# A row of shifts placed by a DMA transfer, score tiles of every fourth target, and side work in other places, in a fused graph-attention layer on one core

## The reference

```python
h = jnp.maximum(_layernorm(x), 0.0)
hs = layer_norm(h, ln1_scale, ln1_bias)            # sources, masked by nodemask
ht = layer_norm(h_target, ln1_scale, ln1_bias)     # targets
q = (ht @ Wq + bq).reshape(T, H, HD) / sqrt(HD)
k = (hs @ Wk + bk).reshape(S, H, HD)
v = (hs @ Wv + bv).reshape(S, H, HD)
logits = einsum('thd,shd->hts', q, k)
logits = where(adj[None] != 0, logits, -1e30)
probs = softmax(logits, axis=-1)
ctx = einsum('hts,shd->thd', probs, v).reshape(T, D)
ht = ht + ctx @ Wo + bo
ht = layer_norm(ht, ln2_scale, ln2_bias)
out = x + ht + gelu(ht @ W1) @ W2
```

## Time and profile before

| | |
|---|---|
| median of 3 runs | 741.07 us (739.25 to 742.01) |
| the profiled execution | 739.28 us, span of its instructions 737.5 us |
| busy, share of the span | PE 91%, DVE 77%, POOL 72%, ACT 61% |
| before unit 0's first score product | 75.66 us |
| units 0 to 31 | 75.66 to 636.57 us |
| behind unit 31 | 100.93 us |

### The profile page before, as it was taken

One profiled execution on the slowest core, in us unless ns is written; L12 is line 12 of the kernel. 1 busy time (PEld: TensorE's weight loads), 2 busy tenths in 40 slices (PEclk: granted clock), 3 DMA queues, 4 the chain that ended last, 5 costly groups with the idle time before them and its releaser, 6 DMA issues.

```text
span 737.5 us, 20293 instructions
## 1 busy us (share of the span) xinstructions
PE 674.4 (91%) x8386; PEld 482.6 (65%) x8386; DVE 569.3 (77%) x962; ACT 450.3 (61%) x806; POOL 533.4 (72%) x504
## 2 busy tenths in 40 slices
PE   4777989999999999969989998799899988889998
PEld 4345656776776777647767766577577756548667
DVE  5858499989889977988899789786677984564651
ACT  4532456666776656667766666775566776775650
POOL 3440299988999977859999688697987998752430
PEclk9999799999999999999999999999999999999999
DMA  8284501103000100210011002020000000000001
GB/s 301 59 246 106 191 30 59 60 31 101 2 2 31 59 30 31 68 63 3 2 59 57 32 31 58 2 97 21 2 2 2 3 2 2 1 1 22 23 16 57
DMA packets 20796, 36.22 MB, mean 49 GB/s; under 512 B 2752, under 2 KB 13280, under 8 KB 20704
## 3 DMA queue, kind: packets, MB, share of 16 engines
q1 hardware_dynamic: 20704, 34.92, 15.1%
HBM read 26.49 MB, written 2.10 MB: 39 GB/s over the span
## 4 chain that ended last, share of the span: by engine, by line
PE 63%; DVE 16%; POOL 10%; issue 6%; ACT 4%; DMA 1%; SPq 0%; DVEq 0%; ACTq 0%
PE score L412 26%; PE early L412 16%; PE ctx L412 12%; POOL prob_lo L1303 7%; DVE early L1100 7%; PE aux L412 7%; DVE prob_lo L1108 3%; ACT prob L817 1%; DVE st_x L1029 1%; POOL w_f L1343 1%; POOL nT L1337 1%; DVE half_max L1100 1%; DVE q_stage L1126 1%; DMA node_i<-in_nodemask 1%; POOL tgt L1307 0%
## 5 line engine op out<-in xcount | busy, mean ns | idle before, releaser
L1303 POOL TENSOR_TENSOR prob_lo<-prob 128x512 f16<-128x512 f32 x384 | 439.9, 1169 | 96.0 <-ACT prob L817 94.8
L817 ACT ACTIVATE prob<-score 128x512 f32<-128x512 f32 x512 | 304.6, 597 | 182.2 <-PE score L412 175.6
L412 PE MATMUL score<-nidentb,mask_nat 128*128 128x128 bf16 x2048 | 201.0, 221 | 9.2 <-ACT prob L817 7.9
L412 PE MATMUL early<-kT,qT 96*128 96x512 f16 x512 | 193.5, 384 | 15.4 <-DVE half_max L1100 15.1
L412 PEld LDWEIGHTS ctx<-v_sb,prob 128*128 128x128 bf16 x2048 | 159.8, 98 | 69.9 <-ACT raw L839 14.6
L412 PE MATMUL ctx<-v_sb,prob 128*128 128x65 f16 x2048 | 192.9, 193 | 10.3 <-POOL prob_lo L1303 5.7
L412 PE MATMUL score<-qT,kT 97*128 97x512 f16 x512 | 198.5, 388 | 0.0
L1100 DVE CUSTOM_DVE_ANT_0 early<-early,mask_nat,half_max 128x1024 f32<-128x1024 f32 x128 | 164.1, 1287 | 43.0 <-PE early L412 41.5
L412 PE MATMUL ctx<-v_sb,prob_lo 128*128 128x65 f16 x2048 | 191.8, 193 | 0.0
L1100 DVE CUSTOM_DVE_ANT_0 early<-early,mask_nat 128x1024 f32<-128x1024 f32 x128 | 156.8, 1231 | 32.1 <-PE early L412 30.7
L412 PEld LDWEIGHTS ctx<-v_sb,prob_lo 128*128 128x128 f16 x2048 | 143.9, 98 | 49.2 <-issue 5.4
(11 more groups left out here) (163 smaller groups left out, 626.9 us busy)
## 6 DMA issues: line engine op xcount, KB each, us to landing
adj_in<-in_adj SPq DMA_DIRECT2D x26, 512.0 KB, 3.8
qT<-q_stage SPq DMA_DIRECT2D x48, 64.0 KB, 2.0
kT<-mask_nat SPq DMA_DIRECT2D x48, 64.0 KB, 2.1
raw<-in_x SPq DMA_DIRECT2D x4, 512.0 KB, 5.6
tgt<-in_L_gnn_h_target SPq DMA_DIRECT2D x4, 512.0 KB, 4.8
prob<-in_adj SPq DMA_DIRECT2D x4, 512.0 KB, 7.4
nT<-in_L_gnn_W SPq DMA_DIRECT2D x2, 1024.0 KB, 8.3
mask_nat<-in_x SPq DMA_DIRECT2D x1, 2048.0 KB, 8.1
```

Source lines behind the costliest of these rows:

```text
L412: return nc.tensor.matmul(dst, w, m, start=start, stop=stop, **more)
L817: nc.scalar.activation(prob[:, n % SLOTS, :], score[n % 2][:, :], ACT.Exp).then_inc(exp_done, 1)
L1303: nc.gpsimd.tensor_tensor(prob_lo[:, n % SLOTS, :], prob[:, n % SLOTS, :], prob_hi(n % SLOTS), ALU.subtract).then_inc(lo_sem["pool"], 1)
```

## The change

It does several things. The row of shifts: the four products and the copy of each unit are gone. ScalarE writes the negated maxima as a compact 128x4 tile (two buffers, by unit parity), and SyncE issues a transfer of it into row 96 of `qT` (`place_shifts`); the next unit's first score product waits for its landing. For the transfer to write the row in order, column `t` of the maxima must hold targets `4*p+t`: the adjacency is loaded so (every fourth row), the early products take every fourth column of `qT` as weights, and the mask products write every fourth column of the score bank.

The side work: in the start, GpSimd masks block 1 of the sources before it norms block 3, the first key projection uses another bank, and the placements are issued head group by head group. `sum_values` stands before unit 0; `up_bias` goes from unit 24 to unit 1; `scale_weight` goes from GpSimd in unit 25 to VectorE in units 2 to 5; `weight_high` and `weight_low` are spread from unit 3 on. Six of the eight mask halves change place, the second norm is one to two units earlier, the turning of the first feed-forward block goes from r = 7 to r = 5. In the last two units VectorE makes eight low halves in place of four. In the tail, turning the last context and multiplying it by Wo are put among the up products.

```diff
-SHIFT_STEP = 8
-MEAN_AT = {(0, 1): 0, (0, 4): 1}
+SHIFT_STEP = 6
-MASK_DVE = [(0, 6), (1, 2), (1, 7), (2, 4), (3, 1), (4, 1), (4, 5), (5, 2)]
+MASK_DVE = [(0, 6), (2, 1), (2, 4), (2, 7), (3, 7), (4, 3), (4, 7), (5, 3)]
+LOAD_AT = [(0, 0), (0, 0), (0, 1), (2, 0), (2, 1), (3, 0), (4, 0), (4, 1)]
-NORM_AT = [(0, 4), (0, 7), (1, 3), (1, 6)]
+NORM_AT = [(0, 5), (1, 1), (1, 3), (1, 5)]
-DVE_LO = (2, 6, 10, 14)
+DVE_LO = [(2, 6, 10, 14)] * (UNITS - 2) + [tuple(range(1, STEPS, 2))] * 2
...
+BIAS_AT = STEPS + 2
...
-                    sp.dma_start(adj_home(k, i), adj[k * TB + t * P:k * TB + (t + 1) * P, h * HALF:(h + 1) * HALF]).then_inc(
+                    sp.dma_start(adj_home(k, i), adj[k * TB + t:(k + 1) * TB:TT, h * HALF:(h + 1) * HALF]).then_inc(
...
+                def place_shifts(u):
+
+                    sp.wait_ge(shift_ready, u + 1)
+                    sp.dma_start(q_block(u // H)[SHIFT_ROW:SHIFT_ROW + 1, u % H, :], shift[:, u % 2, :]).then_inc(shift_in[u % 2], 16)
...
-                    last = mm(early[e % 2][:, i * TB:(i + 1) * TB], q_block(k)[0:ROWS, h, t * P:(t + 1) * P],
+                    last = mm(early[e % 2][:, i * TB:(i + 1) * TB], q_block(k)[0:ROWS, h, t::TT],
...
-                        pe.wait_ge(aux_done, AUX["shift", u] + 1)
+                        pe.wait_ge(shift_in[u % 2], 16 * (u // 2 + 1))
...
-                        mm(score[n % 2][:, t * P:(t + 1) * P], mask_nat[:, k % 2, t, m * P:(m + 1) * P], nidentb[:, :],
+                        mm(score[n % 2][:, t::TT], mask_nat[:, k % 2, t, m * P:(m + 1) * P], nidentb[:, :],
...
-                def shift_row(u):
...
-                    for t in range(TT):
-                        last = mm(aux[0:SHIFT_ROW + 1, t * P:(t + 1) * P], shift[:, t, :], ident16[:, :], True, True)
-                    last.then_inc(aux_ready, 1)
...
-                def row_out(u):
-                    job_here("shift", u)
-                    nc.scalar.activation(q_block(u // H)[SHIFT_ROW:SHIFT_ROW + 1, u % H, :], aux[SHIFT_ROW:SHIFT_ROW + 1, :],
-                                         ACT.Copy).then_inc(aux_done, 1)
...
-                            if r == 5 and s == 15:
+                            if r == 4 and s == 1:
                                 row_deviation(k - 1, lead_width(k - 1))
-                            if r == 6 and s in (2, 4, 7, 11):
+                            if r == 5 and s in (2, 4, 7, 11):
                                 second_norm(k - 1, (2, 4, 7, 11).index(s))
...
-                            if r == 5 and 3 <= j < 3 + TT:
+                            if r == 3 and 3 <= j < 3 + TT:
                                 lead_stats(k - 1, j - 3, j == 2 + TT)
-                            if r == 6 and j == 1:
+                            if r == 4 and j == 2:
                                 lead_scale(k - 1, lead_width(k - 1))
```

More of the change, by code:

```diff
@@ L77, in aux_job @@
     k, r = divmod(u, H)
[L78 to L81, removed]
     if k + 1 < NTB and (r, s) in QT_AT:
@@ L102, in aux_numbers @@
 def aux_numbers():
-    jobs = [("shift", 0)] + [aux_job(u, s) for u in range(UNITS) for s in range(STEPS) if aux_job(u, s)]
+    jobs = [("mean", 0), ("mean", 1)] + [aux_job(u, s) for u in range(UNITS) for s in range(STEPS) if aux_job(u, s)]
     jobs += [("cT", NTB - 1, c) for c in range(DC)] + [("wo", NTB - 1, i) for i in range(TT // 2)]
@@ L120, in pairs_at, with lo_counts @@
     return range(first, min(first + 1, UNITS * PAIRS))
[L123 to L128, removed]
+def lo_counts():
+    count, done = {"dve": 0, "pool": 0}, []
+    for n in range(TILES):
+        who = "dve" if n % STEPS in DVE_LO[n // STEPS] else "pool"
+        count[who] += 1
+        done.append((who, count[who]))
+    return done
+LO_DONE = lo_counts()
 def lo_here(u, j):
-    first = [m for m in DVE_LO if m < 3] if u == 0 and j == 0 else []
-    soon = [u * STEPS + m for m in range(2 * j + 3, 2 * j + 5) if m % STEPS in DVE_LO]
-    return first + [n for n in soon if n < TILES]
+    first = [n for n in range(3)] if u == 0 and j == 0 else []
+    soon = range(u * STEPS + 2 * j + 3, u * STEPS + 2 * j + 5)
+    return [n for n in [*first, *soon] if n < TILES and LO_DONE[n][0] == "dve"]
 def adj_use(k, i):
@@ L299, in prob_hi, with proj_bank @@
             return prob[:, slot, :].bitcast(BF16).rearrange("p (t two) -> p t two", two=2)[:, :, 1]
+        def proj_bank(g, m):
+            return early[0][:, m * TB:(m + 1) * TB] if g == 1 else (ctx, aux)[m][:, :]
         def value_bank(i):
@@ L666, in _ @@
                             early_scores(e, s % 2)
-                        if aux_job(u, s) == ("shift", u + 1):
-                            shift_row(u + 1)
-                        if k == 0 and (r, s) in MEAN_AT:
-                            sum_values(MEAN_AT[r, s])
+                        if n == BIAS_AT:
+                            up_bias()
                         if k + 1 < NTB:
@@ L925, in _ @@
                     high_values(i)
+                act.wait_ge(q_first, FIRST)
+                act.wait_ge(q_placed[0], REST)
+                for g in range(2):
+                    mean_out(g)
                 negated(0)
-                row_out(0)
                 for n in range(AHEAD):
```

230 lines of the change are left out of this document (126 added, 104 removed).

## The result

The changed kernel takes 801.13 us, median of 4 runs (800.13 to 801.39), beside 740.63 for the kernel before, measured with it: a ratio of 1.0814 [1.0791, 1.0837], slower. The forecast of 712 fell; the time is that of the first rival, 797. In the profiled execution the span grew from 737.5 to 799.6 us.

The account below looks back on a forecast made before the run. TensorE was taken to bound a plain unit (14.91 us), other engines some units. Against the profiled 739.28 us the terms summed to -26.9, giving 712 us; its own range was 700 to 726, stretched to 806 to include half-rate mask products.

Parts of the forecast that it names:

- first rival: Mask products of every tile run at half rate: 0.20 us a tile over 512 tiles, total 797 us; chance 0.36.
- The stride in PSUM and in the weights: Mask products writing, and early weights read, every fourth column: taken to cost nothing, though called the weak point.
- tight spots of the queue: Next block's shift row, behind query placements at r = 5, lands slightly late: 0.5 on each of three, +1.5 us.
- start, to the first score product: Before unit 0: shorter TensorE stream, but first shift row behind 60 placements; -1 us, between +3 and -3.
- unit 0: First unit loses the two mean sums, 16 products of 256 columns each, on busy TensorE: -3 us.
- units 1 and 2: `up_bias` enters unit 1 (19.9 us), three mask halves and weight scaling fill unit 2 (18.1): +5 us.
- units 3 to 7: Weights' low halves on GpSimd, 1.2 us each, raise it to 15.0 against 14.9: nothing, with the shift's saving.
- blocks 1 and 2: Middle blocks: mask halves, norms, statistics and square root change units; -3.7 and -4.6, together -8.3 us.
- units 24 to 27: Last block's first half: unit 24 loses `up_bias` (-4.3 us), unit 25 two scalings (-4.9), the other two -0.4.
- units 28 to 31: Last four units fall from 63.5 to 56.5 us, the final two having nearly no early products: -7.0.
- tail: After the last unit: turned-context work among the up products removes about 4.5 of 6.7 us TensorE idle: -4.5.
- The wait on the transfer: Each unit's shift row lands in 2.0 to 2.6 us, hidden within 3.3, except three tight places: +1.5 us.

Follow-up runs that it names:

- experiment 1: Kernel after, with the four mask products writing 128 neighbouring columns of the score bank again, transfers and strided early weights kept: 726.98 us, ratio 0.9807.
- experiment 3: Kernel before, with only the mask products changed to write every fourth column of the score bank: 817.14 us, ratio 1.1016.
- experiment 8: Kernel after, with the four shift products and the copy put back and tiles in the order of before, leaving the moved work alone: 723.74 us, ratio 0.9767.
- experiment 11: experiment 8 with the tail of before put back: 722.77 us, ratio 0.9735.

## Why the prediction was wrong, and where it was right

The forecast fell by one step, "The stride in PSUM and in the weights": "I take nothing, since the mask, score and early products all go at the column rate of their clock". None of those rows has a gap in its output, so they could say nothing on it, and the Trainium skill's rule that was cited against the choice is the one that held for this stride. Measured it is 0.18 for four mask products and 0.03 on the score product behind them, 74 us in all, from experiments 1 and 3. The range of 700 to 806 holds the 801 only because it had been stretched to the rival; the forecast itself had the wrong sign.

Rival 1 had the mechanism, with 0.20 a tile, and its plain unit of 17.9 is the 17.94 measured. That its 797 comes so near is in part luck. It stands on the 712, which is 15 below the 727 of the kernel without the stride, and it adds 85 for the stride, which is 11 above the 74: it took 17 of 102 as hidden, where the runs show 21.7 of 95.9 by busy times and some 33 of 107 by the spacing of starts. The other half of the step was right: the weights' stride costs nothing that shows.

The rest can be read in experiments 1 and 8, which have the moved work without the stride. The table gives differences to the profiled execution of before in us, by the borders of units; the three measured columns each sum to the difference of the spans, but for rounding. The start of experiment 1 is its first score product at 79.70.

| stretch | forecast | exp. 1 (transfer) | exp. 8 (products) | after |
|---|---|---|---|---|
| tight spots of the queue | +1.5 | in the units | in the units | in the units |
| start, to the first score product | -1 | +4.0 | -1.3 | +4.2 |
| unit 0 | -3 | -2.5 | -4.7 | -0.1 |
| units 1 and 2 | +5 | +4.0 | +6.4 | +8.3 |
| units 3 to 7 | 0 | +2.9 | +3.9 | +13.7 |
| blocks 1 and 2 | -8.3 | -8.2 | -7.7 | +28.5 |
| units 24 to 27 | -9.6 | -9.3 | -8.5 | +1.4 |
| units 28 to 31 | -7.0 | -5.4 | -5.6 | +3.8 |
| tail | -4.5 | +2.4 | +2.3 | +2.4 |
| sum | -26.9 | -12.1 | -15.1 | +62.1 |

Point by point:

- *Start.* Mis-sized. In the kernel after 45 placements took 31.93, 0.71 each where the step had 0.66, the last ended at 75.2 and not at 71.3, and the row landed in 4.0, not 2 to 3. The row waits for its place in the queue, not for its data: ScalarE had negated the maxima at 71.5, and in experiment 8, where no queue is in the way, the first score product starts at 74.37.
- *The wait on the transfer.* Right in the main: 1.9 to landing in the median, and the tight spots at r = 5 didn't bite. But not every row is so quick. In experiment 1, whose units have about the forecast length, two later rows took 3.6 and 3.1 to land, and TensorE waited 0.3 and 0.9 for them; the step had 3.3 us to hide in.
- *Units 1 and 2.* The sum was near, its parts were not: unit 1 took 20.7 and 23.2 for 19.9, unit 2 16.0 and 15.9 for 18.1. The 32 products of `up_bias` took 3.63 in experiment 1, as before the change, and 5.39 in experiment 8, where the granted clock fell to 0.50 while they ran and stayed there for 6 us. What differs is when the clock falls and for how long; why that differs between the two wasn't tested.
- *Units 3 to 7.* "Nothing" was wrong. The step added one low half to 13.79, GpSimd's time in a plain unit, and left out the rest that the change puts there: a piece of the weights' scaling on VectorE in each of units 3 to 5 (0.48 to 1.33 us a piece in experiment 1, where the step of units 1 and 2 had 0.5), and a second mask half in unit 5. These are units 3 and 5 in experiment 1:

```profile
142.57:159.96 17.39, 16.14 (x237) 11.68 (x235) 16.44 (x23) 11.53 (x22) 14.83 (x13) 1.00 0.12 33
...
178.35:195.59 17.24, 15.49 (x229) 10.63 (x227) 17.24 (x24) 10.54 (x21) 15.99 (x14) 1.00 0.20 48
```

  Before they took 15.82 and 16.34, with VectorE busy in 14.98 and 15.94. Unit 5 is now VectorE's throughout; in unit 3 no engine is full. Which of the pieces costs how much wasn't tested.
- *Blocks 1 and 2.* The sum was right by offsets (its items as written add to -8.5, not -8.3). These windows of experiment 1 show them: r = 1, r = 4 and r = 6 of block 1, units 24 and 25, and the tail.

```profile
240.75:258.53 17.78, 15.34 (x229) 10.77 (x227) 17.78 (x27) 10.03 (x19) 17.78 (x17) 1.00 0.12 32
...
295.90:315.55 19.65, 18.34 (x237) 12.34 (x235) 18.87 (x30) 14.12 (x25) 13.06 (x13) 1.00 0.20 56
...
332.62:347.66 15.04, 14.74 (x229) 10.88 (x227) 14.00 (x22) 10.42 (x21) 14.36 (x13) 1.00 0.02 2
496.87:511.45 14.58, 14.58 (x229) 10.83 (x227) 13.72 (x20) 10.01 (x19) 14.58 (x14) 1.00 0.26 78
511.45:528.13 16.68, 15.52 (x229) 10.82 (x227) 16.68 (x24) 10.03 (x20) 16.68 (x16) 1.00 0.24 78
...
622.09:725.40 103.31, 94.61 (x640) 64.84 (x638) 51.08 (x86) 52.25 (x83) 32.40 (x36) 0.98 0.06 21
```

  r = 6 is 15.04, as forecast; r = 4 rose by 1.3 where 1.8 was forecast. r = 1 was forecast at 16.0 and is 17.8, with VectorE and GpSimd both full: two mask halves less brought nothing there. Unit 24 is 14.6 for a forecast of 15.7, and unit 25 16.7 for 15.5.
- *Tail.* Wrong in sign. The step took TensorE's 2.55 of idle time ahead of the context's turning for a gain. The timeline of TensorE in experiment 1 shows what came in its place:

```profile
638.07 4.45 PE L452 MATMUL score<-qT,w_f 128*128 128x512 f16 x12 [3.37 <-DVE qT L1187]
664.14 3.12 PE L452 MATMUL early<-w_f,kT 128*128 128x256 f16 x27 [1.60 <-DVE adj_in L1298]
```

  TensorE's busy time there is nearly the same (94.61 for 94.26), but it idles 8.7 for 6.7. The up products of the second block wait 3.37 for VectorE's low half of that block (`normed_low`), and the down products 1.60 for a result (`y_done`). Experiment 11, with the old order, has neither wait among its own; it has the 2.56 for the turned context and 1.41 behind it. That the loss comes from the new order is argued from these rows and experiment 11's profile, and the times alone don't prove it.

So the change without its stride is worth 12 us by the profiled executions and 14 by the ratio (experiment 1), not the 27 forecast. The moved work alone is worth 17 (experiment 8, 2.3%), and the new way of placing the row nothing by itself, or a little less; the stride that it needs costs 74.

## What to carry to other kernels

Before a layout is changed to save a few small instructions, look at every product that will write or read it with a step: here four products and a copy a unit (0.33 us of a unit) were bought with 16 tiles at 0.21 to 0.22 more each. A row in which a pattern does not occur is no evidence that it is free; when all of the trace is silent, a stated rule about it should weigh more than the silence. If elements must be interleaved in PSUM, keep neighbours in pairs of fp32, each beginning at an even column as here; and where a transfer takes over from an engine, count where it will stand in its queue at the start of the kernel, not only how long it flies.

## What the runs showed that was not expected

- A bf16 product that writes 128 fp32 columns to PSUM with a step of 2 or 4 columns goes at half the pace (four in 0.40 us for 0.22), while pairs with gaps go at the full one. At a granted clock of 0.50 the step of 4 costs in proportion (0.74 for 0.40). The weight loads behind the strided products grow from 99 to 140 ns.
- The moving operand in fp16 with a step of 8 bytes halves the pace (0.44 for 0.22 us for 512 columns); with 4 bytes it costs 0.01. As weights the step of 8 bytes showed no cost.
- 32 products of one column took 3.6 us in three kernels (the kernel after, experiment 1) and 5.39 in experiment 8, with the granted clock at 0.50 in all of 104 to 110 us. Groups of 8 took 0.95 and, once the clock was at 0.50, 1.7, and splitting them so didn't help.
- 128 pieces of 8 bytes into one partition landed in a median of 1.9 us, and in 3.1 to 4.0 at times; four transfers of 128 pieces of 2 bytes, one behind the other, took a median of 4.9 each.
